# Last stage of a graph network: features in two float32r pieces instead of three bf16 ones, and the adjacency kept in fp32

## The reference, cut to what matters

```
h = relu(layernorm(x))
x = x + L2(h):  h = relu(h @ W_self0.T + mean_neigh(h) @ W_neigh0.T + b0)
                h =      h @ W_self1.T + mean_neigh(h) @ W_neigh1.T + b1
h = relu(layernorm(x))
x = x + L3(h):  three times
                h = layernorm(relu(sum_e(h[src]@W * dinv[src]*dinv[dst]) + self loop + b)) * g + be
                widths 128 -> 256 -> 256 -> 128
```

## Time and profile before

| what | us |
|---|---|
| median of 3 runs | 3906.61 (3905.37 to 3919.26) |
| the profiled execution: its own time | 3927.33 |
| its span in the trace | 3925.3 |
| TensorE (PE) busy | 3393.5, 86% |
| VectorE (DVE) busy | 1826.2, 47% |
| GpSimd (POOL) busy | 1781.0, 45% |
| ScalarE (ACT) busy | 1453.8, 37% |
| mean DMA rate | 172 GB/s |
| chain that ended last | PE 16%, of it line 3193 14% of the span |

### The profile page before, as it was taken

The page is one execution under the profiler, slowest core; times in us unless marked ns, Lnnn a source line. Parts: engine busy times, 40 slices in busy tenths (PEclk is TensorE's granted clock), DMA queues, the critical chain, the costliest instruction groups (busy, mean ns, idle before and its releaser), DMA issues. The chain is left out here.

```text
span 3925.3 us, 81257 instructions
## 1 busy us (share of the span) xinstructions
PE 3393.5 (86%) x22381; PEld 2072.9 (53%) x22381; DVE 1826.2 (47%) x5337; ACT 1453.8 (37%) x3467; POOL 1781.0 (45%) x1807
## 2 busy tenths in 40 slices
PE   4999999994875999999699989679888879999998
PEld 1566666662553555655355545345454535555554
DVE  4566666665854444453344444334444332353222
ACT  3555555552243454544233333223333331132122
POOL 1444444551015777774677777377777600000000
PEclk8988889996987999999889998789999989999999
DMA  3566666664836566665778787487777644543133
GB/s 116 170 186 192 187 184 185 178 177 80 255 116 176 157 183 176 184 178 133 201 208 223 217 229 200 118 228 208 203 205 207 164 151 171 177 153 109 55 116 123
DMA packets 717221, 675.09 MB, mean 172 GB/s; under 512 B 383123, under 2 KB 543738, under 8 KB 716810
## 3 DMA queue, kind: packets, MB, share of 16 engines
q1 hardware_dynamic: 623290, 466.05, 40.5%
q0 software_dynamic: 77008, 200.24, 18.9%
q10 hardware_dynamic: 16768, 6.91, 0.7%
HBM read 530.63 MB, written 142.28 MB: 171 GB/s over the span
## 5 line engine op out<-in xcount | busy, mean ns | idle before, releaser
L2190 POOL DMA_INDIRECT l_y<-s_lrows,l_src x1332 | 1331.9, 1000 | 456.7 <-issue 383.7
L3193 PE MATMUL ps<-nl_adj,nl_table 126*128 126x504 bf16 (+1 forms) x3150 | 631.2, 357 | 2.3 <-DVE nl_table L3428 2.3
L951 POOL DMA_INDIRECT em_gs<-s_rows,em_idx x400 | 389.6, 974 | 424.6 <-DMA em_idx<-in_sd 312.4
L3193 PEld LDWEIGHTS ps<-nl_adj,nl_table 126*128 126x128 bf16 x3150 | 301.8, 96 | 298.7 <-issue 5.0
L2230 PE MATMUL ps<-ident,l_y 128*128 128x128 f32 x1800 | 268.0, 285 | 205.7 <-DMA l_y<-s_lrows,l_src 124.1
L2273 PE MATMUL ps<-l_y,aw_pT 128*63 128x277 f32 x2700 | 384.8, 423 | 2.5 <-ACT aw_pT L2467 2.0
L2584 DVE TENSOR_TENSOR l_y<-l_y 128x768 f32<-128x768 f32 x225 | 214.0, 951 | 331.5 <-DMA l_y<-s_lrows,l_src 288.2
L2453 ACT ACTIVATE aw_yT<-ps 128x512 f32<-128x512 f32 (+1 forms) x525 | 262.0, 534 | 256.5 <-PE ps L2230 245.9
L2257 PE MATMUL ps<-aw_yT,aw_qt 128*63 128x384 f32 x1800 | 338.4, 499 | 6.9 <-DMA aw_yT<-s_dxT 6.9
L2230 PEld LDWEIGHTS ps<-ident,l_y 128*128 128x128 f32 x1800 | 205.2, 144 | 263.5 <-issue 201.8
L2619 DVE COPY aw_axd<-ps 128x252 f32<-128x252 f32 x225 | 94.6, 420 | 410.0 <-PE ps L2290 392.9
(11 more groups left out here) (375 smaller groups left out, 5872.9 us busy)
## 6 DMA issues: line engine op xcount, KB each, us to landing
nl_adj<-s_adj SPq DMA_DIRECT2D x20, 3100.8 KB
aw_yT<-s_dxT SPq DMA_DIRECT2D x150, 384.0 KB, 4.4
aw_geoS<-s_geoS SPq DMA_DIRECT2D x450, 94.5 KB
nl_adj<-s_adj SPq DMA_DIRECT2D x15, 2325.6 KB
ws_msg<-s_msg SPq DMA_DIRECT2D x75, 384.0 KB, 3.9
s_dxT<-aw_yT SPq DMA_DIRECT2D x75, 384.0 KB, 4.4
aw_qt<-s_qt SPq DMA_DIRECT2D x225, 126.0 KB
s_msg<-em_msg SPq DMA_DIRECT2D x100, 256.0 KB, 2.5
```

The source lines that it names most:

```text
L951: pool.indirect_dma_start(out=gs[:, u, j, :], out_offset=None, in_=d["rows0"], in_offset=bass.IndirectOffsetOnAxis(ap=idx[:, u, 2 * j:2 * ...
L2190: pool.indirect_dma_start(out=y[:, u, j, 0:W], out_offset=None, in_=table, in_offset=bass.IndirectOffsetOnAxis(ap=src[:, u, j:j + 1], axis ...
L3193: m = nc.tensor.matmul(k.ps[:, bank(i, p), 0:cols * WN], source[:, p, q, b, :], adj[:, a % 2, 0:cols, b * WN:(b + 1) * WN], start=b == 0 a ...
```

## The change

The features are cut in two pieces instead of three. VectorE masks the low 12 bits of each fp32 number (MASK), subtracts the rest (LO, written as float32r), and ScalarE copies the masked number (HIGH, float32r); REST and MID are gone. The tables, the adjacency in the last stage and the small identity are float32r, and each aggregation product has two pieces. The adjacency is stored in fp32 in two DRAM tensors (15 and 10 source blocks), laid out so that one piece is 5 source blocks (`PB`) of all windows of a turn: a run of up to 10,080 bytes per partition. A turn loads five such pieces into a ring of four; a slot is free again when the products of its piece are done (`consumed`). The order of products in a turn is by piece, then part, then block. The path that would store bf16 and cast it on GpSimd is there, but with both types F32 it issues nothing. In `em` the counts are copied by two ScalarE instructions and stored by two DMAs per window, in runs of 840 bytes.

```diff
+PB = 5
+ADJ_BLOCKS = (15, 10)
+ADJ_TYPES = (F32, F32)
+PIECES = tuple((bank, n) for bank in range(2) for n in range(ADJ_BLOCKS[bank] // PB))
+TOP12 = -4096
...
 em: oh_key, iota_key: 2 * 13 * HN = 546 columns -> 525; counts: 273 + 273 columns -> 315 + 210
-                sp.dma_start(d["adj"][bass.ds(i * NWI + v, 1), :, :].rearrange("w p c -> (w p) c"),
-                             adj[:, v, 0:NB, :].rearrange("p b n -> p (b n)")).then_inc(adj_out[v], 16)
+                for q in range(2):
+                    sp.dma_start(d[f"adj{q}"][:, :, bass.ds(i * NWI + v, 1), :].rearrange("n p w c -> p (n w) c"),
+                                 adj[q][:, v, :, :].rearrange("p (n b) m -> p n (b m)", b=PB)).then_inc(adj_out[v], 16)
...
-                nc.scalar.activation(adj[:, v, :, h * HN:(h + 1) * HN]..., k.ps[0:BM, ADJ:ADJ + 2, 0:KN]..., ACT.Copy)
+                for q in range(2):
+                    nc.scalar.activation(adj[q][:, v, :, h * HN:(h + 1) * HN], k.ps[0:BM, ADJ + q, 0:KN[q]]..., ACT.Copy)
...
-        table = [sb("table0", [BM, 1, 3, NB, D], BF16), sb("table1", [BM, 2, 3, NB, D], BF16)]
-        adj = sb("adj", [BM, 2, AW, NB * WN], BF16)
+        table = [sb("table0", [BM, 1, 2, NB, D], F32R), sb("table1", [BM, 2, 2, NB, D], F32R)]
+        RING, RAW = 4, 3
+        adj = sb("adj", [BM, RING, AW, PB * WN], F32R)
...
 load(i), on SyncE; before: load(AHEAD) first of all, then the small loads, then the rest;
 after: the small loads, then
+            for i in range(AHEAD, len(turns)):
+                for p, (bank, at) in enumerate(PIECES):
+                    g = NP_ * (i - AHEAD) + p
+                    if g >= RING:
+                        sp.wait_ge(consumed, g - RING + 1)
+                    sp.dma_start(adj[:, g % RING, 0:n, :].bitcast(F32), d[f"adj{bank}"][at, :, w:w + n, :])
...
-                order = ([(p, b) for p in range(parts) for b in range(late)] +
-                         [(p, b) for p in range(parts) for b in range(late, NB)])
+                order = [(n, p, b) for n in range(NP_) for p in range(parts) for b in range(n * PB, (n + 1) * PB)]
+                for at, (n, p, b) in enumerate(order):
+                    if p == 0 and b == n * PB: wait for piece g = NP_ * a + n
                     if c == 0 and p == 0 and b in FIRST:
+                        pe.wait_ge(act_.sem, act_.of(i - AHEAD + FIRST.index(b), "HIGH"))
                         pe.wait_ge(dve_.sem, dve_.of(i - AHEAD + FIRST.index(b), "LO"))
-                    for q in range(3):
+                    for q in range(2):
...
-                    if was != "x" and n == (8 if was == "c1" else 2):
+                    if was != "x" and at == (12 if was == "c1" else 3):
                         make(i - 1)
-                    if was == "n0" and n == 14:
+                    if was == "n0" and at == 20:
                         turn(i - 1)
-                    if was == "c3" and n == 18:
+                    if was == "c3" and at == 23:
                         turn(i - 1)
-                    if was == "c2" and n == (30 if kind == "c2" else 19):
+                    if was == "c2" and at == (45 if kind == "c2" else 19):
                         turn(i - 1)
-                    if was == "c2" and n == (38 if kind == "c2" else 20):
+                    if was == "c2" and at == (49 if kind == "c2" else 20):
                         mix(i - 1)
...
 ScalarE: HIGH copies the masked rows; MID is gone
+                    act.wait_ge(dve_.sem, dve_.of(i, "MASK"))
+                    nc.scalar.activation(hi, top_, ACT.Copy).then_inc(s, 1)
...
 VectorE: REST and LO become
+                dve.wait_ge(act_.sem, act_.of(i - 1, "HIGH"))
+                nc.vector.tensor_scalar(top_.bitcast(I32), src.bitcast(I32), TOP12, None, ALU.bitwise_and).then_inc(s, 1)
+                after("MASK")
+                nc.vector.tensor_tensor(lo, src, top_, ALU.subtract).then_inc(s, 1)
```

More of the change, by code:

```diff
@@ L9 @@
 I16 = mybir.dt.int16
+F32R = mybir.dt.float32r
 ALU = mybir.AluOpType
@@ L3056, in centred, with top, summed, loaded @@
             return (xc, t)[i % 2][:, 0:SIZES[turns[i][1]], 0:D]
-        def beyond_high(i):
+        def top(i):
             return rest[:, 0:SIZES[turns[i][1]], i % 2 * D:(i % 2 + 1) * D]
+        NP_ = len(PIECES)
+        DIRECT = [ADJ_TYPES[bank] == F32 for bank, _ in PIECES]
+        def summed(i):
+            return NP_ * (i - AHEAD + 1)
+        def loaded(g):
+            return sum(DIRECT[h % NP_] for h in range(g % RING, g + 1, RING))
+        def casts(g):
+            return g // NP_ * DIRECT.count(False) + DIRECT[:g % NP_].count(False)
         def goes_to(kind):
@@ L3103, in _ @@
                 sp.dma_start(w2[:, p, :], d["gW2"][p * D:(p + 1) * D, :]).then_inc(w_in, 16)
-            load(AHEAD + 1)
-            for i in range(AHEAD + 2, len(turns)):
+            for i in range(AHEAD, len(turns)):
                 load(i)
@@ L3198, in aggregate @@
+                    if b % PB == PB - 1 and p == parts - 1:
+                        m.then_inc(consumed, 1)
                     if b == 0 and kind in LOOPS:
                         for j in range(SIZES[c]):
-                            for q in range(3):
+                            for q in range(2):
                                 nc.tensor.matmul(k.ps[:, bank(i, p), j * BM:(j + 1) * BM], source[:, p, q, FIRST[c] + j, :],
-                                                 idb[0:BM, 0:BM], start=False, stop=False)
+                                                 idr[:, :], start=False, stop=False)
@@ L3308, in deviation @@
                 nc.scalar.activation(std[:, i % 2, 0:nb], squares[:, i % 2, 0:nb], ACT.Sqrt, bias=k.eps[0:BM, 0:1], scale=1.0 / D).then_inc(s, 1)
-            def middle(i):
-                act.wait_ge(dve_.sem, dve_.of(i, "REST"))
-                nc.scalar.activation(table[0][:, 0, 1, blocks(turns[i][1]), :], beyond_high(i), ACT.Copy).then_inc(s, 1)
             def high(i):
-                act.wait_ge(dve_.sem, dve_.of(i, "Y"))
-                nc.scalar.activation(table[0][:, 0, 0, blocks(turns[i][1]), :], rows_of(i), ACT.Copy).then_inc(s, 1)
+                act.wait_ge(dve_.sem, dve_.of(i, "MASK"))
+                nc.scalar.activation(table[0][:, 0, 0, blocks(turns[i][1]), :], top(i), ACT.Copy).then_inc(s, 1)
             keep(0)
```

166 lines of the change are left out of this document (86 added, 80 removed).

## The result

The changed kernel is slower: 4090.4 us (median of 4 runs, 4031.8 to 4111.6) against 3906.0 (median of 4) for the kernel before. Two of the four runs (4108.5 and 4111.6) fell in a slower state of the chip, so the ratio, 1.036 with an interval of 1.028 to 1.043, is that of the other two (4031.8 and 4072.3) to the kernel before. The forecast was 3807. The profiled execution took 4072.3 us (span 4070.4), the one before 3927.3 (3925.3). The difference of the spans, 145.1 us, is what the two traces have to explain.

A forecast was written before the change was run, and what follows sets the result against it. TensorE was taken to bound the last stage (busy 716.0 of 728.0 us). Terms -15 - 6.6 - 10.6 - 53 - 19 + 4 = -100 us gave 3827 profiled, 3807 as median; range 3750 to 3865 for eight in ten.

The forecast's parts named there:

- Bytes: Adjacency loads of the last stage: 39.7 MB a layer at 366 GB/s, so 17.35 us per four-block turn.
- +92.5 for -15: Layers n0 and n1: bound by the loads, with VectorE starting c1 at 3424 instead of 3439.3, a gain of 15 us.
- The edge stage: Stage that writes the adjacency: doubled stores and bytes, split ScalarE copies, mostly covered by TensorE; +4 us.
- rival E: The writing stage is dearer or the clock falls: +60 us, 3867 us in all; chance 0.10.
- The float32r product: Aggregation products of 504 columns: one pass at the bf16 price of 0.217 us, 2100 products instead of 3150.
- C: Rival: the float32r product runs at two cycles a column, 0.43 us, giving 4100 us; chance 0.10.
- D: Rival: each float32r product waits for its weights, 0.31 to 0.33 us, giving 3900 to 3925 us; chance 0.06.
- The loops: Loop products on TensorE, 8 instead of 12 a turn and part: 0.11 us each, +0.2 us a part.
- step c2: Layer c2: loads hidden, four-block turns 30.0 us and three-block 22.9, including 0.9 and 0.5 added; gain 53 us.
- c1, "17.9": Layer c1: the chain loses MID and its gap, so turns fall from 19.0 to 17.9 us; gain 6.6 us.
- The 10.6 us of c2's first turn: Behind c1's last link, 37 positions of two products remain instead of 41 of three: 16.1 for 26.7 us.
- step c3: Layer c3: first turn 22.4 us where it was 26.8, then 80 us set by the loads; gain 19 us.

The follow-up runs named there:

- b_twice: Kernel before with each adjacency load followed by a second load of nearly the same bytes, two in flight; n0 and n1 ended 328 us after the first TAKE.
- b_serial: Kernel before with the same double loads as b_twice, but one in flight; n0 and n1 ended 271 us after the first TAKE.
- e_mix: Changed kernel with the first 15 of 25 adjacency blocks stored in bf16 and cast to float32r by GpSimd; 3890.4 us, ratio 0.991.
- e_bf16: Changed kernel with the whole adjacency stored in bf16 and cast to float32r by GpSimd; 3921.5 us, ratio 1.0005.
- e_few: Changed kernel with four fifths of the aggregation products left out and all loads kept, output not the reference's; 3994.2 us.
- a_one: Changed kernel with each piece's load issued only once the piece before has landed, one in flight; 195 GB/s at a DMA share of 0.57.
- run 329: Not a run of its own: 329 is the GB/s that b_twice, the kernel before with doubled adjacency loads, moved in c3.

## Why the prediction was wrong

**The step that failed is Bytes, "I take 366".** The rate was read from a stretch "in which only one such load ran", and applied to a ring in which up to four are in flight. The step asked whether longer runs could be slower and not what the queue would look like. Measured: 264 GB/s (252 over n0, 244 over n1) and four-block turns of 23.6 to 29.9 us in n0 and n1 instead of 17.35. The bounds of the rate, 349 and 388, were both of lone loads, so the range could not hold the result. The first load did leave when forecast, 10.3 us into the stage (11 forecast). This step carries the misses of n0 and n1 (+92.5 for -15), of c3 (+24.4 for -19), and most of c1. b_twice against b_serial shows, for n0 and n1, that loads in flight together moved less. Why they slow each other there stays open, and so does why they did not in c3 of b_twice (329 GB/s at a share of 0.91) and in e_mix (277 at 0.77).

**The edge stage, "+4".** Measured +55.3. The split copies take 0.43 and 0.34 us where one took 0.636, so 0.14 more each time and not 0.25; with the doubled number of stores they belong to the 13.5 us of e_bf16. What the step left out is the fp32 bytes, some 42 us. With them go longer waits of TensorE for VectorE's em_a (between 100 and 905 us 49.9 us before, 47.4 in e_bf16, 57.0 in e_mix, 72.5 in the changed kernel) and a lower granted clock (0.93, 0.93, 0.91, 0.89). The DMA share doesn't tell them apart (0.63, 0.69, 0.68, 0.67), and what makes em_a late is open. This was in rival E, at 0.10. Only 37 of it arrive at the last stage.

**The float32r product, "I take 0.217".** The stretch of c2 in which nothing waits, in the form of the earlier trace rows:

```profile
3714.43 18.66 PE L3239 MATMUL ps<-nl_adj,nl_table 126*128 126x504 f32 x76
3732.93 1.00 PE L3247 MATMUL ps<-nl_idr,nl_table 126*128 126x126 f32 x8
3733.77 1.66 PE L3239 MATMUL ps<-nl_adj,nl_table 126*128 126x504 f32 x6
```

(3732.93 - 3714.43)/76 = 0.243 us: one pass, as forecast, with 0.026 on top. C and D need 0.31 and more and fall. The weight load's record is 186 ns at best where bf16's was 96, and lies under the product before it. The loops, taken at 0.11, cost 0.84/8 = 0.105 us each. A four-block turn of c2 has 100 products (two parts, 25 blocks, two pieces), so the 0.026 on top make 2.6 us: 30.0 + 2.6 = 32.6, and measured are 3830.79 - 3798.57 = 32.2, the same in e_bf16 and e_mix. The product price is the whole miss of these turns; the 0.5 us that step c2 added for a new wait did not come, since TensorE does not wait in such a turn (it does in the three-block ones, some 0.5 us before the product with W2). Two of the four-block turns lost 7.8 us each and one 6.3: the one large gain that arrived.

**c1, "17.9".** Measured 19.5 to 19.7 in turns 4 and 5. The mechanism was right: HIGH (3649.68, 1.06 us) and TAKE (3650.65) stand back to back, and the mask takes 0.69, not 1.22. What the step missed is that W1's product stands in TensorE's order behind products that wait for a load:

```profile
3648.82 2.06 PE L3239 MATMUL ps<-nl_adj,nl_table 126*128 126x378 f32 x10 [0.66 <-DMA nl_adj<-s_adj]
3652.26 1.36 PE L3239 MATMUL ps<-nl_adj,nl_table 126*128 126x378 f32 x6 [1.39 <-DMA nl_adj<-s_adj]
3653.46 1.89 PE L3187 MATMUL ps<-nl_w,nl_sums 128*126 128x256 f32 x8
```

TAKE ended at 3651.22, and W1 began 2.2 us later. The 10.6 us of c2's first turn did not come either: its TAKE is 29.6 us after c1's last, 30.1 before. TensorE waited for nothing in these 29.6 us. The part that the step counted did shrink: from the start of the last W1 product to that TAKE it is 19.3 us where it was 28.9. But W1 stands behind the first positions of c2 in TensorE's order. Before, those were done while the chain ran, and W1 began 1.2 us after c1's last TAKE (3544.18); now TensorE came to them only at 3702.32, with a granted clock of 0.50 until 3707, and W1 began 10.3 us after the TAKE at 3703.03. Before, then after:

```profile
3545.37 1.46 PE L3145 MATMUL ps<-nl_w,nl_sums 128*126 128x256 f32 x6
```

```profile
3702.32 1.18 PE L3239 MATMUL ps<-nl_adj,nl_table 126*128 126x504 f32 x2 [3.05 <-issue]
...
3713.32 1.46 PE L3187 MATMUL ps<-nl_w,nl_sums 128*126 128x256 f32 x6
```

In step c3 the 26.8 us given for the first turn of before is 26.1 by its TAKE; nothing in the sum used it.

The measured 4090 lies beside rival C's 4100; that is chance, its mechanism did not occur. The clock (0.84 in n1) fell with the waits, but e_few, at 0.55, had turns no longer.

## What to carry to other kernels

A rate read where one load is alone in the queue is the rate of one load alone: before doubling the bytes, divide GB/s by the share in a stretch that has as many loads in flight as the new kernel will have, or make one by loading twice. Several loads in flight are not slow in every layer, so only such a trial tells. Where loads go one by one, split them only as far as a gap of 2 to 2.6 us per load (a_one) is hidden. A change that gives TensorE a third less work pays only in the layers whose loads have slack (here c2, two parts to a load); storing small counts in a wide type costs twice, at the store and at each load.

## What was not expected of the hardware

In n0 and n1 two loads in flight together moved less (216 GB/s) than the same two one after the other (251 GB/s, gaps included), and in c3 of the same run 329. A float32r product of 504 columns takes 0.243 us, 12% more than bf16's 0.217. A GpSimd cast of 126x2520 takes 2.44 us on average in e_bf16, and beside such casts a VectorE pass of 126x512 with both operands in SBUF takes 1668 ns for 692.
